# Moving projections between the stages of a pipelined attention and mixture-of-experts kernel

## The reference, cut to what matters

```python
# B=8, S=512, D=256, 16 heads of 16; E=8 experts, top 2, hidden F=704
x = x + tanh(g_xattn) * cross(layernorm(x), ctx, ctx)      # softmax(q k^T / 4) v per head, no projections
n = layernorm(x)
h = n + attention(rmsnorm(n, g1), wq, wk, wv, wo)          # q, k rotated (RoPE), causal
y = h + moe(rmsnorm(h, g2), w_router, wg, wu, wd)          # (silu(t wg) * (t wu)) wd over each token's 2 experts
x = x + tanh(g_ffn) * y
```

## Time and profile before

| | us |
|---|---|
| median of 3 runs | 1590.68 |
| lowest, highest | 1581.02, 1591.45 |
| the profiled execution | 1575.98 |
| its span, first to last instruction | 1573.6 |
| mean granted clock of TensorE | 0.976 of full |
| busy: TensorE, VectorE, ScalarE, GpSimd | 1433.8, 975.2, 777.3, 879.7 |

### The profile page before, as it was taken

One profiled execution on the slowest core, in us unless ns is written; L12 is line 12 of the kernel. 1 busy time (PEld: TensorE's weight loads), 2 busy tenths in 40 slices (PEclk: granted clock), 3 DMA queues, 4 the chain that ended last, 5 costly groups with the idle time before them and its releaser, 6 DMA issues.

```text
span 1573.6 us, 31721 instructions
## 1 busy us (share of the span) xinstructions
PE 1433.8 (91%) x9439; PEld 881.3 (56%) x9439; DVE 975.2 (62%) x2329; ACT 777.3 (49%) x1782; POOL 879.7 (56%) x1147
## 2 busy tenths in 40 slices
PE   3999999999999999999899998845999999999997
PEld 1232334344444444444444454434999999999996
DVE  5888767757767766766866656324555555555553
ACT  1576665665665664665566555611333333333332
POOL 7485776974977977877879676533222222222222
PEclk9999999999999999999999999957999999999999
DMA  7665356565565574664553646146252454355220
GB/s 198 187 173 174 106 177 180 169 209 143 153 204 166 167 218 148 180 181 163 175 187 103 210 136 192 68 166 207 38 150 53 136 151 143 47 152 149 40 42 11
DMA packets 116517, 230.19 MB, mean 146 GB/s; under 512 B 20101, under 2 KB 82949, under 8 KB 114310
## 3 DMA queue, kind: packets, MB, share of 16 engines
q1 hardware_dynamic: 76114, 147.65, 31.2%
q0 software_dynamic: 26032, 69.82, 15.8%
q10 hardware_dynamic: 14212, 10.71, 2.7%
HBM read 135.10 MB, written 93.14 MB: 145 GB/s over the span
## 4 chain that ended last, share of the span: by engine, by line
PE 68%; POOL 9%; DVE 8%; issue 5%; ACT 4%; DMA 4%; SPq 1%; ACTq 0%; POOLq 0%; DVEq 0%
PE pv_ps L984 9%; PE pv_ps L713 9%; PE max_ps L689 9%; PE key_ps L689 9%; PE max_ps L946 8%; PE key_ps L963 8%; DVE neg L1274 4%; PE aux L1032 3%; PE aux L1023 3%; ACT probs L1155 2%; PE turn_ps L702 2%; PE aux L1016 2%; POOL rows_in L1681 2%; DMA q_stack<-neg_rows 2%; POOL w_parts L1578 1%
## 5 line engine op out<-in xcount | busy, mean ns | idle before, releaser
L1274 DVE TENSOR_REDUCE neg<-max_ps 128x1 f32<-128x512 f32 (+3 forms) x864 | 543.5, 666 | 278.9 <-PE max_ps L949 177.3
L1155 ACT ACTIVATE probs<-key_ps 128x512 f32<-128x512 f32 (+3 forms) x1024 | 497.1, 519 | 366.8 <-PE key_ps L963 176.1
L946 PE MATMUL max_ps<-k_stack,q_stack 96*128 96x512 bf16 (+3 forms) x1024 | 356.1, 352 | 30.8 <-DVE neg L1274 16.2
L963 PE MATMUL key_ps<-q_stack,k_stack 99*128 99x512 bf16 (+3 forms) x1024 | 350.3, 343 | 24.4 <-ACT probs L1155 16.0
L556 POOL DMA_INDIRECT out<-part,whose x71 | 110.1, 1551 | 377.4 <-DVE part L589 304.9
L946 PEld LDWEIGHTS max_ps<-k_stack,q_stack 96*128 96x128 bf16 x1024 | 100.8, 99 | 219.3 <-DVE neg L1274 123.0
L963 PEld LDWEIGHTS key_ps<-q_stack,k_stack 99*128 99x128 bf16 x1024 | 100.2, 98 | 131.0 <-ACT probs L1155 70.0
L713 PE MATMUL pv_ps<-weights,hidden_t 128*128 x1207 | 161.9, 288 | 1.4 <-DVE hidden_t L609 1.4
L689 PE MATMUL max_ps<-weights,rows_t 128*128 x642 | 153.7, 385 | 2.8 <-DVE rows_t L580 2.8
L689 PE MATMUL key_ps<-weights,rows_t 128*128 x636 | 150.3, 381 | 1.0 <-DVE rows_t L580 1.0
L713 PEld LDWEIGHTS pv_ps<-weights,hidden_t 128*128 128x128 f32 x1207 | 149.0, 191 | 1.7 <-issue 1.7
(11 more groups left out here) (213 smaller groups left out, 2102.1 us busy)
## 6 DMA issues: line engine op xcount, KB each, us to landing
w_split<-w_parts POOLq DMA_DIRECT2D x32, 704.0 KB, 5.6
weights<-w_split SPq DMA_DIRECT2D x8, 2816.0 KB
weights<-w_split SPq DMA_DIRECT2D x8, 1280.0 KB
rows<-rows_in ACTq DMA_DIRECT2D x71, 129.0 KB, 2.1
w_split<-w_parts POOLq DMA_DIRECT2D x16, 512.0 KB, 3.6
kept_sb<-kept SPq DMA_DIRECT2D x16, 512.0 KB, 6.1
parts_cross_k<-parts_k SPq DMA_DIRECT2D x48, 128.0 KB
parts_cross_q<-parts_q SPq DMA_DIRECT2D x48, 128.0 KB
```

The source lines that it names most:

```text
L946: r = mm(ps[:, 0:keys], q_stack[g][0:KROWS, hd, qt * P:(qt + 1) * P], k_stack[g][0:KROWS, hd, 0:keys], start=True, stop=not own)
L963: r = mm(ps[:, q0:S], k_stack[g][0:KROWS + NEGROWS, hd, kt * P:(kt + 1) * P], q_stack[g][0:KROWS + NEGROWS, hd, q0:S], start=True, stop=no ...
L1155: act.activation(probs[:, kt % 2, hd, q0:S], key_ps[j % 2][:, q0:S], ACT.Exp).then_inc(m["exp_done"], 1)
L1274: v.tensor_reduce(neg[:, g % 2, hd - place_:hd + 1, qt], scores, op=ALU.max, axis=AX.X, negate=True).then_inc(m["max_red"], many)
```

## The change

It rewrites the tables and a few places of the code; what is computed stays.

- Keys: from places 105 and 117 of step b-1 (slots 6 and 7) to 10 and 24 of step b (slots 0 and 1). Queries: from 80 and 85 (slot 5) to 112 and 120 (slot 7). The second value half: from slot 2 to 3. The attention's transposes and the output projection: from slots 3 and 4 to 5 and 6. The transposes of hn1: from slot 4 to 5.
- The first residual's second half and its end: from slot 0 of the next step to slot 7.
- Routing (HN2_TURNS to PLACES): from step b+1, slots 5 to 7, to step b+2, slots 4 to 6. GpSimd's hn2 rows and base rows stay in step b+1 and go to slot 7; scatters go to step b+3.
- The weight pieces of a step: from 0, 0, 0, 2, 3, 2, 1, 0 by slot to 0, 0, 0, 1, 2, 1, 3, 1.
- `turned` and `with_cos` are one place each for queries and keys.
- hn1_t and hn2_t are copied out of PSUM by VectorE (`take_out`) and not by ScalarE.
- The maxima's rows are sent by SyncE (`send_neg`), once per slot, at a place of its queue written out by hand.
- The last steps have places of their own.

```diff
-HN1_TURNS = {b: at(b - 1, 72, 76) for b in REGULAR_OWN} | {0: at(0, 4, 8), LAST - 1: at(LAST - 2, 44, 48), LAST: at(LAST - 1, 4, 8)}
-Q_HALVES = {b: at(b - 1, 80, 85) for b in REGULAR_OWN} | {0: at(0, 12, 17), LAST - 1: at(LAST - 2, 52, 57), LAST: at(LAST - 1, 12, 17)}
-K_HALVES = {b: at(b - 1, 105, 117) for b in REGULAR_OWN} | {0: at(0, 22, 27), LAST - 1: at(LAST - 2, 82, 87), LAST: at(LAST - 1, 22, 27)}
+HN1_TURNS = {b: at(b - 1, 92, 95) for b in REGULAR_OWN} | {0: at(0, 4, 8), LAST - 1: at(LAST - 2, 46, 50), LAST: at(LAST - 1, 4, 8)}
+Q_HALVES = {b: at(b - 1, 112, 120) for b in REGULAR_OWN} | {0: at(0, 12, 17), LAST - 1: at(LAST - 2, 54, 59), LAST: at(LAST - 1, 12, 17)}
+K_HALVES = {b: at(b, 10, 24) for b in REGULAR_OWN} | {0: at(0, 26, 34), LAST - 1: at(LAST - 2, 78, 83), LAST: at(LAST - 1, 26, 34)}
...
+STEP_PIECES = (0, 0, 0, 1, 2, 1, 3, 1)
...
-            turned = {"q": s1("turned_q", DC, S), "k": s1("turned_k", DC, S)}
-            with_cos = {"q": s1("with_cos_q", DC, S), "k": s1("with_cos_k", DC, S)}
+            turned, with_cos = s1("turned", DC, S), s1("with_cos", DC, S)
...
+                def send_neg(step, s):
+                    unit = step.neg_of(s)
+                    if unit:
+                        n = unit[2] * G + unit[3]
+                        sp.wait_ge(m["neg_ev"], n + 1)
+                        sp.dma_start(q_stack[unit[3]][KROWS:KROWS + NEGROWS, :, :], neg_rows[:, :]).then_inc(m["neg_dma"], 16)
...
                     load_stack(step.half(0), 1)
+                    send_neg(step, 0)
                     if i + 3 < B:
                         load_ctx(i + 3)
...
                     load_stack(step.half(0), 2)
+                    send_neg(step, 1)
...
                                 act.activation(neg_rows[:, :], turn_b[0:NEGROWS * HG * QT, 0:P], ACT.Copy).then_inc(m["neg_ev"], 1)
-                                step.wait(act, m["neg_ev"], n + 1)
-                                act.dma_start(q_stack[ng[3]][KROWS:KROWS + NEGROWS, :, :], neg_rows[:, :]).then_inc(m["neg_dma"], 16)
...
                     k = 2 * "qk".index(o) + c
                     aux_full(dve, o, b, c)
-                    over(dve, m["rope_used"], 4 * (b - 1) + k + 1)
+                    over(dve, m["rope_used"], 4 * b + k - 1)
...
+                def take_out(name, b, c, dst, scale):
+                    aux_full(dve, name, b, c)
+                    v.tensor_scalar(dst[:, c, :], aux[:, :], scale[:, c:c + 1], None, ALU.mult).then_inc(m["aux_free"], 1)
```

More of the change, by code:

```diff
@@ L167 @@
+XQ_STAGE = {b: stage(b - 4, 5) if b > 3 else stage(-1, 4 if b == 3 else 2) for b in range(2, B)}
 X_STAGE = {1: stage(-1, 0), 2: stage(-1, 4), **{b: stage(b - 3, 2 + (b == 3)) for b in range(3, B)}}
@@ L818, in first_step @@
                     load_x(2)
+                    send_neg(step, 1)
                     store_parts("q", "x", 1)
+                    send_neg(step, 2)
                     store_parts("k", "c", 1)
@@ L854, in body @@
                     load_stack(step.half(0), 2)
+                    send_neg(step, 1)
                     if not in_halves:
                         keep(i + 1)
+                    if i == LAST - 1:
+                        send_base(i - 2)
                     if i:
@@ L865, in body @@
                     load_stack(step.half(1), 0)
+                    send_neg(step, 3)
                     if i + 4 < B:
@@ L874, in body @@
                     load_stack(step.half(1), 1)
+                    send_neg(step, 4)
                     if i + 3 < B:
@@ L877, in body @@
                     load_stack(step.half(1), 2)
+                    send_neg(step, 5)
                     if i == LAST - 2:
@@ L881, in body @@
                     load_stack(step.half(1), 3)
+                    send_neg(step, 6)
                     if i == LAST - 2:
@@ L886, in body @@
                         load_stack(step.half(2), 0)
+                    send_neg(step, 7)
                     if 0 < i < LAST - 1:
@@ L1083, in extra @@
                         b, _, _ = logits[u]
-                        aux_free(pe, "hn2", b, DC - 1)
+                        aux_turn(pe, "lg", b, 0)
                         for t in range(QT):
@@ L1162, in evacuate @@
                         .then_inc(m["aux_free"], 1)
-                x_turns, c_turns, hn1_turns, att_turns, hn2_turns = (times(t) for t in (X_TURNS, C_TURNS, HN1_TURNS, ATT_TURNS, HN2_TURNS))
+                x_turns, c_turns, att_turns = (times(t) for t in (X_TURNS, C_TURNS, ATT_TURNS))
                 hn1_rows, v_halves, h_squares, choices = times(HN1_ROWS, 2), times(V_HALVES), times(H_SQUARES, QT), times(CHOICES)
@@ L1378, in place @@
                         v.tensor_scalar(token[:, :], token[:, :], float(S), None, ALU.add).then_inc(m["route"], 1)
+                def take_out(name, b, c, dst, scale):
+                    aux_full(dve, name, b, c)
+                    v.tensor_scalar(dst[:, c, :], aux[:, :], scale[:, c:c + 1], None, ALU.mult).then_inc(m["aux_free"], 1)
                 def extra(u):
+                    if u - 2 in hn1_turns:
+                        b, c, _ = hn1_turns[u - 2]
+                        if b:
+                            aux_full(dve, "v", b - 1, DC - 1)
+                        take_out("hn1", b, c, hn1_t, g1_sb)
+                    if u - 2 in hn2_turns:
+                        b, c, _ = hn2_turns[u - 2]
+                        take_out("hn2", b, c, hn2_t, g2_sb)
                     if u - 3 in q_halves:
@@ L1504, in _ @@
                 aux_free(dve, "c", 0, 0)
-                split(flat_k, parts["k"], 0, turned["k"], "c_parts", 0)
+                split(flat_k, parts["k"], 0, turned, "c_parts", 0)
                 for c in range(DC):
                     aux_free(dve, "x", 0, c)
-                    split(flat_q, parts["q"], c, turned["q"], "x_parts", 3 * c)
+                    split(flat_q, parts["q"], c, turned, "x_parts", 3 * c)
                 dve.wait_ge(m["ld_sq"], 16)
```

93 lines of the change are left out of this document (48 added, 45 removed).

## The result

The changed kernel took 1620.99 us in the median (1617.51 to 1626.94, 4 runs) against 1589.92 for the kernel before: a ratio of 1.0218, 95% interval 1.0187 to 1.0249 (the kernel before has one run more here than in the table ahead of the prediction, so 1589.92 and not 1590.68). Run again beside the experiments it gave 1.0244 (1.0205 to 1.0283). The forecast was 1572, its range 1550 to 1597; the measured time lies above it. Its profiled execution has a span of 1620.8 us, 47 more than that of before; by the ratio it is 35, since the profiled execution of before was among its shortest.

A forecast was written before the change was run, and what follows sets the result against it. TensorE was taken as the bound. Moved work 0.0, SyncE sending -12.8 and late maxima -6.2 gave -19.0, less 1 us for GpSimd's extra piece: -18, from 1590.7 to 1572 us, range 1550 to 1597.

The forecast's parts named there:

- the slower rivals: Two cases above the forecast: shared rotation places with a late GpSimd (1607, chance 0.09), maxima late behind SyncE's queue (1596, 0.06).
- The bound: TensorE bounds the kernel; moving instructions can give back at most part of its 53 us idle from 134.5 to 997.9 us.
- Keys: Both key halves move from slots 6, 7 to 0, 1: 2.1 us a half there, bounds 1.4 and 3.6; net +0.2 a step.
- three units apart instead of four: Transposes standing closer together after the moves of queries, values, output projection and attention's transposes: +0.6 us a step.
- First residual: Second half of the sum and its statistics leave slot 0 (-1.3 us) for slot 7 (+0.6): net -0.7 a step.
- Evacuations: Four scaled copies a step (hn1, hn2) go from ScalarE to VectorE, out of slots 4 and 5: -1.2 us a step.
- Routing one step later: Moving routing adds a group to step 6 and takes one from step 1: zero.
- SyncE sends the maxima: ScalarE loses 64 issues of 0.73 us; 0.2 us a slot taken, -12.8 us in all, bounds 0 and 46.7.
- The fourth rival: Maxima come late behind SyncE's queue in slots 0 and 1, 1.5 us each in 8 steps: +24 us, 1596; chance 0.06.
- Late maxima: Levelled weight pieces end waits for GpSimd's split; steps 1 to 4 lose their excess over the shortest: -6.2 us.
- The third: Shared rotation places and an extra GpSimd piece delay slots 0 and 1 by 2.9 us each: +35 us, 1607; chance 0.09.
- the first rival: Nothing comes of the change, as TensorE is the bound; only the late maxima go: 1585 us; chance 0.25.

The follow-up runs named there:

- a_both: Changed kernel, context's turns of steps 1 to 4 at units 30 and 34, extras of steps 5 and 6 at least 4 units apart: 1599.92 us, 1.0128 of before.
- a_apart: Changed kernel with only the context's turns of steps 1 to 4 moved to units 30, 34 and the first value half to 39: 1613.01 us, 1.0207 of before.
- best1b: Kernel before with SyncE sending the maxima and GpSimd's weight pieces levelled over slots 4 to 7, run once more: 1562.81 us, 0.9891 of before.

## Why the prediction was wrong, step by step

The time lies outside the range and on the side of the slower rivals, which had small chances; neither of them is what happened.

**The bound** was read right: TensorE is it. But that a change of places "can give back part of these 53 us and no more" says only what can be won. The idle time grew to 82, and with it the busy time by 19, mostly as clock, for which the sum had no term. One reading of the earlier trace rows is off, without a consequence: TensorE's idle time in a slot reaches 1.2 us, not 1.3.

**Keys, the step that failed first.** "I take 2.1, near TensorE's row, since three score banks let VectorE work while TensorE projects." A half in slot 0 costs 3.6, exactly the upper end of its bounds, TensorE's part and VectorE's one after the other. The edit came to +14 us alone (a move of five batches, with the context's turn close behind) where the sum had +0.2 a step. Taken out of slots 6 and 7 the two halves gave back 5.0 together, against the 4.0 taken. This step alone would not have left the range: at 3.6 a half the sum is 2 x 1.5 x 5 = 15 us more, 1587. What took it outside is the next step, and the terms below that gave less than was taken (the sender 3.8 of 12.8).

**The distances weren't a term at all.** The prediction names transposes "three units apart instead of four" and gives 0.6 a step for them, but never asked what a turn three units behind a *projection* does, which leaves one unit between. It measured 1.96 us a step in slot 1, and the places that a_both moved, with the half clock behind them, 18 us of the whole. For the transposes three units apart, 0.6 was too little: in slot 5 TensorE waits 1.6 to 2.0 us a step for the bank. The rows that tell it stand in the order of the changed kernel, not in any trace of before.

**First residual.** -1.3 in slot 0 and +0.6 in slot 7 were taken; -1.1 and +1.4 are measured. The error is slot 7, where VectorE was busy for 11.7 of 13.8 us already.

**Evacuations.** -1.2 a step came out of rows that show a wait of 5.4 us over the whole run. Measured: nothing in slots 4 and 5, and 2 to 10 us lost overall.

**Routing one step later.** It "adds a group to step 6 and takes one from step 1: zero." It is -4.2 and +7.9; that the last score step is the more crowded one is the likely reason, which no run took apart.

**SyncE sends the maxima.** 0.2 a slot, 1.6 a step, was met in step 4 (1.5), but not in the other steps. As a whole it came to 3.8 and not 12.8; that GpSimd's split was next in line accounts for 2.7 us of the difference. The fourth rival didn't happen: in the steps of the profiled kernels in which SyncE sends, the score product waits for the maxima's transfer 0.5 us at most. The rule on ring order that the prediction drew from the Trainium skill ("DMA: Bandwidth & Descriptors", Queues, rings and completion order) would let the stack loads delay the maxima; no run here shows such a delay.

**Late maxima.** -6.2 was taken for the levelled pieces. They give 9.4 alone (5.7 to 13.2) and, by difference, some 13 to 16 beside the sender. In the changed kernel the waits for the split fell from 7.3 us in five places to the one of 3.6 in step 6, so this part seems to have worked and to be buried under the rest; no run took it out there.

**The rivals.** The third had the sign, the slots (0 and 1) and not the cause: VectorE waits for GpSimd twice, 3.2 us in sum, in step 5 alone; giving queries and keys a place each again took the wait away and gained nothing. ScalarE waited for the xn rows 0.6 us in slot 1. Of the signs set out in the prediction, slot 2 under 15.5, slot 4 under 16 and slot 7 over 15 held; slots 0 and 1 at 14 to 15 (15.2 and 17.2), no slot over 17 (two at 17.2) and steps at 117 to 120 (123 to 128) didn't. The sign against the first rival, idle time that falls, didn't hold either.

What stays open: the parts measured alone are keys 14 to 24, routing 4, residual 2 to 6, evacuations 2 to 10, sender and pieces -17 to -20. Of the keys some 7 us hang on the distance to the context's turn (a_apart, steps 1 to 4), which a_both has set right. So the parts sum to between -5 and 20 us for a_both, which measured 20, and up to 25 are not assigned. The regular steps 2 to 4 of a_both take 124.5 us against 119.4 in best1b; in step 4 slots 0 and 1 are 2.2 and 3.8 us longer, slots 5 and 7 are 1.2 and 1.7 longer, and slots 2, 4 and 6 give back 3.9. Slot 5 is where the turns three units apart stand. The new places of queries, attention and output projection were not tried alone.

## What to carry to other kernels

Where two engines hand one bank to each other in a stage in which both are busy (in slot 0 before, VectorE for 94% and TensorE for 93% of the time), price an added operation as the sum of both parts: 2.2 + 1.4 us cost 3.6. Check the distance to the bank's next user in the new order, not in the old trace. When an edit's local gain is real but the total isn't, look for the engine that is late next and try both edits together: 3.8 and 9.4 us alone were 17 to 20 together here.
